# Mixture of experts a slot earlier, with scatters, gathers and additions at places of their own

## What is computed

```
xn = layernorm(x)
x = x + attention(xn)            # 16 heads of 64, causal, softmax of q.k / 8, output projection
      + experts(xn)              # 8 experts, each token goes to its 2 best

gate = softmax(xn @ Wg);  top-2 scores, divided by their sum
expert e: (g * sigmoid(g) * v) @ W2[e]   with g = xn @ W11[e], v = xn @ W12[e]
out  = score0 * expert_out[idx0] + score1 * expert_out[idx1]
```

## Time and profile before

| | |
|---|---|
| time, median of 3 runs | 1510.97 us (1510.51 to 1512.25) |
| the profiled execution's own time | 1510.68 us |
| its span, first to last instruction | 1508.8 us |
| granted TensorE clock, mean | 0.943 |
| DMA moved over the span | 36.23 MB, mean 24 GB/s |
| POOL's indirect DMAs | 32 scatters (median 971 ns on POOL), 32 gathers (median 997 ns) |

### The profile page before, as it was taken

One profiled execution on the slowest core, in us unless ns is written; L12 is line 12 of the kernel. 1 busy time (PEld: TensorE's weight loads), 2 busy tenths in 40 slices (PEclk: granted clock), 3 DMA queues, 4 the chain that ended last, 5 costly groups with the idle time before them and its releaser, 6 DMA issues.

```text
span 1508.8 us, 26916 instructions
## 1 busy us (share of the span) xinstructions
PE 1322.1 (88%) x9090; PEld 1007.4 (67%) x9090; DVE 1080.6 (72%) x3370; ACT 762.2 (51%) x1645; POOL 286.5 (19%) x393
## 2 busy tenths in 40 slices
PE   3289999999999999889977948699999999999961
PEld 2167777777777676656555727577888888888751
DVE  3688888989898887462258836478777787777643
ACT  2325465555546464543324525366666666666540
POOL 4000000000000000000033245322222222222224
PEclk9679999999999999989988978899999999999986
DMA  2000000000000000100003010200111111210002
GB/s 96 0 1 1 2 1 1 1 2 2 1 1 2 1 1 1 44 1 0 0 0 84 1 63 24 69 1 1 58 57 57 57 57 57 57 57 8 17 20 56
DMA packets 39538, 36.23 MB, mean 24 GB/s; under 512 B 2288, under 2 KB 38128, under 8 KB 39152
## 3 DMA queue, kind: packets, MB, share of 16 engines
q1 hardware_dynamic: 37360, 30.36, 6.7%
q0 software_dynamic: 2048, 4.20, 1.0%
HBM read 26.17 MB, written 8.39 MB: 23 GB/s over the span
## 4 chain that ended last, share of the span: by engine, by line
PE 47%; issue 6%; DVE 3%; POOL 3%; DMA 2%; ACT 1%; another core or an unknown queue 1%; SPq 0%; POOLq 0%; DVEq 0%; ACTq 0%
PE PS L2182 8%; PE PS L2168 8%; PE PS L2109 4%; PE PS L2160 4%; PE PS L2161 4%; PE PS L2195 4%; PE PS L2202 3%; PE PS L2239 2%; PE PS L2129 2%; PE PS L1804 2%; PE PS L2210 2%; PE PS L2249 1%; PE PS L2009 1%; PE PS L2027 1%
## 5 line engine op out<-in xcount | busy, mean ns | idle before, releaser
L1035 ACT ACTIVATE pe_<-PS 128x512 f32<-128x512 f32 (+3 forms) x384 | 177.6, 488 | 160.1 <-PE PS L2012 119.3
L1102 ACT ACTIVATE PN<-PS,NM 128x128 f32<-128x128 f32 (+7 forms) x256 | 189.0, 739 | 109.7 <-DVE NM L1708 69.3
L1708 DVE CUSTOM_DVE_ANT_0 PS<-PS,mask_row 128x128 f32<-128x128 f32 (+7 forms) x256 | 194.2, 765 | 67.0 <-PE PS L2161 58.8
L2160 PE MATMUL PS<-KA,QA 128*128 128x512 f32 (+3 forms) x384 | 159.0, 415 | 55.9 <-issue 41.0
L2168 PE MATMUL PS<-ident,PN 128*128 128x128 f32 x1152 | 179.1, 278 | 9.1 <-issue 2.6
L2168 PEld LDWEIGHTS PS<-ident,PN 128*128 128x128 f32 x1152 | 137.0, 143 | 48.3 <-issue 36.8
L1989 PE MATMUL PS<-kta,qta 128*128 128x512 f32 (+3 forms) x384 | 148.2, 421 | 5.7 <-DVE tmqs L1421 2.3
L2009 PE MATMUL PS<-qtb,kta 128*128 128x512 f32 (+3 forms) x384 | 138.9, 389 | 0.9 <-ACT pe_ L1035 0.9
L2161 PE MATMUL PS<-KB,QA 128*128 128x512 f32 (+3 forms) x384 | 130.7, 353 | 0.0
L1421 DVE CUSTOM_DVE_ANT_0 PS<-PS,W 128x128 f32<-128x128 f32 (+3 forms) x256 | 124.8, 496 | 3.6 <-PE PS L1989 2.2
L2160 PEld LDWEIGHTS PS<-KA,QA 128*128 128x128 f32 x384 | 75.2, 196 | 71.9 <-issue 52.4
(11 more groups left out here) (294 smaller groups left out, 2919.4 us busy)
## 6 DMA issues: line engine op xcount, KB each, us to landing
W<-w SPq DMA_DIRECT2D x40, 384.0 KB, 4.1
W<-by_expert SPq DMA_DIRECT2D x10, 256.0 KB, 4.7
expert_out<-YS SPq DMA_DIRECT2D x10, 256.0 KB, 2.3
W<-w SPq DMA_DIRECT2D x1, 2508.0 KB, 10.9
by_expert<-WOZ SPq DMA_DIRECT2D x2, 1024.0 KB, 6.8
W<-w SPq DMA_DIRECT2D x1, 1536.0 KB, 5.8
X<-x SPq DMA_DIRECT2D x2, 512.0 KB, 4.9
out<-X SPq DMA_DIRECT2D x1, 1024.0 KB, 5.0
```

The lines of the kernel that those rows point to most:

```text
L1035: act.activation(pe_[:, h, n % 2, 0:w], PS[:, 4 + h % 2, 0:w], ACT.Exp, scale=HD0 ** -0.5)\
L1102: act.activation(prob_rows(u, r), scores_of(u), ACT.Exp, bias=NM[:, u:u + 1], scale=-1.0, accum_out=SM[:, r % 2, u:u + 1]).then_inc(score_ ...
L1708: dve.tensor_tensor_reduce(scores_of(u), scores_of(u), mask_row[:, S - w:S], -HD1 ** -0.5, -MASKED, ALU.add, ALU.min, NM[:, u:u + 1]).then ...
L2160: pe.matmul(piece, query, KA[:, b, h, lo:lo + n], start=True, stop=False)
```

## The change

The expert batches run from slot 4 instead of 5. The router starts in slot -1 (`gate0+`) and makes four steps after each item instead of one. The scatters are an item `send0` at the end of POOL's order, in three portions of 12, 12 and 8, in the slots 1, 2 and 3, each with one wait for the landing of all so far. The gathers are an item `fetch0'`: sixteen for batch 0 of the tokens in slot 14, sixteen for batch 1 in slot 15, each portion with waits for all its landings. The second half of `YG` lies over the expert weights, so no gather waits for additions. The additions are items `cm0'` to `cm7'` of DVE in slot 16, each with four additions (two tiles, first halves and then second halves). The result is stored in two DMAs of 512 KB.

```diff
-        YG = XM
+        YG = [XM, W1[:, lo_:lo_ + NT * D].rearrange("p (t d) -> p t d", t=NT)]
-        PE1 = steps1("gate0 S0 T14.1' md0' ... S7 gate1' k1+ T5.0 ...
+        PE1 = steps1("S0 T14.1' md0' ... S7 k1+ gate0+ T5.0 S8 T4.0 T6.0 v1+ S9 mu2 S10 gate1 w6' T7.0 w4' ...
-        DVE1 = steps1("gate0 mx13' x0' tc11.1' x2' mx14' mx15' ql1 zc1' mx0 mx1 qr1+ kd1 mx2 kr0+ mx3 tc15.1' mh1 mx5 "
-                     "tc0.0 mx4 gate1 tc1.0 ql0+ zc2' mx6 mh0 mx7 mx8 gate2' tc6.0 kd0+ mx9 mh2 x6' mx10 x4' mx11 "
-                     "tc9.1 tc9.0 mx12 mh3")
+        DVE1 = steps1("mx13' x0' tc11.1' x2' mx14' mx15' cm0' ql1 zc1' cm1' mx0 mx1 qr1+ kd1 mx2 gate1 kr0+ mx3 tc15.1' "
+                     "cm2' mh1 mx5 tc0.0 mx4 tc1.0 ql0+ zc2' cm3' cm4' cm5' mx6 mh0 mx7 mx8 tc6.0 kd0+ gate0+ mx9 mh2 "
+                     "x6' cm7' mx10 x4' cm6' mx11 gate2 tc9.1 tc9.0 mx12 mh3")
-        POOL1 = steps1("kh1' qh1' kh0 qh0 kl0 kl1'")
+        POOL1 = steps1("kh1' qh1' kh0 qh0 kl0 kl1' send0 fetch0'")
-        MOE_FROM, BATCHES, DISPATCH_FROM = 5, TILES1 // 4, 3
+        MOE_FROM, BATCHES = 4, TILES1 // 4
+        ROUTER_STEPS = 4
+        SENDS = [12, 12, 8]
+        ONCE = {"send": range(MOE_FROM - 3, MOE_FROM), "fetch": range(MOE_FROM + BATCHES - 1, MOE_FROM + BATCHES + 1),
+                "cm": (ROUNDS - 1,)}
+            def send(n):
+                pool.wait_ge(routed, 1)
+                pool.wait_ge(slots_cleared, 48)
+                upto = sum(SENDS[0:n + 1])
+                for i in range(sum(SENDS[0:n]), upto):
+                    pool.indirect_dma_start(... XM[:, i // 2, :] ...).then_inc(dispatched, 16)
+                pool.wait_ge(dispatched, 16 * upto)
+            def fetch(b):
+                pool.wait_ge(y_stored, 16 * BATCHES)
+                for t in range(TB * b, TB * (b + 1)):
+                    for k in range(2):
+                        pool.indirect_dma_start(YG[b][:, 2 * (t % TB) + k, :], ... ).then_inc(fetched[t], 16)
+                for t in range(TB * b, TB * (b + 1)):
+                    pool.wait_ge(fetched[t], 32)
+                elif kind == "cm":
+                    for t in (2 * item[1], 2 * item[1] + 1):
+                        after(dve, ("x", t % TB // 2 * 2), ROUNDS - 2 + t // TB)
+                        dve.wait_ge(fetched[t], 32)
+                        dve.scalar_tensor_tensor(X[:, t, :], YG[t // TB][:, 2 * (t % TB), :], w_two[:, t, 0:1], X[:, t, :],
+                                                 ALU.mult, ALU.add).then_inc(half_combined, 1)
+                    for t in (2 * item[1], 2 * item[1] + 1):
+                        halves[0] += 1
+                        dve.wait_ge(half_combined, halves[0])
+                        dve.scalar_tensor_tensor(... 2 * (t % TB) + 1 ...).then_inc(combined[t // TB], 1)
+                for _ in range(ROUTER_STEPS):
+                    if not held:
+                        held = next(router, None) in ("exp", "prefix")
+            for b in range(B):
+                sp.wait_ge(combined[b], TB)
+                sp.dma_start(out[b * S:(b + 1) * S, :] ..., X[:, b * TB:(b + 1) * TB, :]).then_inc(stored, 16)
```

More of the change, by code:

```diff
@@ L519, in rounds @@
                         if r == 0:
+                            yield item, r
+                    elif item[0] in ONCE:
+                        if r in ONCE[item[0]]:
                             yield item, r
@@ L542, in program @@
             sem("m1_tokens_by_act"), sem("m1_tokens_by_dve"), sem("m1_out_by_act"), sem("m1_out_by_dve"))
-        slots_cleared, dispatched, y_stored, combined = (
-            sem("m1_slots_cleared"), sem("m1_dispatched"), sem("m1_out_stored"), sem("m1_combined"))
+        slots_cleared, dispatched, y_stored, half_combined = (
+            sem("m1_slots_cleared"), sem("m1_dispatched"), sem("m1_out_stored"), sem("m1_half_combined"))
+        combined = two("m1_combined")
         weights_in, tokens_in = two("m1_weights_in"), two("m1_tokens_in")
-        fetched = [sem(f"m1_fetched_{k}") for k in range(8)]
+        fetched = [sem(f"m1_fetched_{t}") for t in range(NT)]
         done1 = {}
@@ L552, in counts @@
             for item, r in rounds(steps):
-                if item[0] == "gate":
+                if item[0] == "gate" or item[0] in ONCE:
                     continue
@@ L753, in _ @@
                          YS[:, :].rearrange("p (c d) -> p c d", c=4)).then_inc(y_stored, 16)
-            sp.wait_ge(combined, 2 * NT)
-            sp.dma_start(out.rearrange("(t p) d -> p t d", p=P), X[:, :, :]).then_inc(stored, 16)
-            sp.wait_ge(stored, 16)
+            for b in range(B):
+                sp.wait_ge(combined[b], TB)
+                sp.dma_start(out[b * S:(b + 1) * S, :].rearrange("(t p) d -> p t d", p=P), X[:, b * TB:(b + 1) * TB, :])                    .then_inc(stored, 16)
+            sp.wait_ge(stored, 32)
         @block.gpsimd
@@ L899, in _ @@
                 link(pool.memset(KB[head_rows(1 - h), :, h, :].bitcast(F32), 0.0))
-            def dispatch():
+            def send(n):
                 pool.wait_ge(routed, 1)
                 pool.wait_ge(slots_cleared, 48)
-                for t in range(NT):
-                    for k in range(2):
[L907 to L914, removed]
+                upto = sum(SENDS[0:n + 1])
+                for i in range(sum(SENDS[0:n]), upto):
+                    pool.indirect_dma_start(
+                        by_expert[:, :], bass.IndirectOffsetOnAxis(idx[:, i // 2, i % 2:i % 2 + 1], 0), XM[:, i // 2, :],
+                        None, bounds_check=SLOTS - 1, oob_is_err=False).then_inc(dispatched, 16)
+                pool.wait_ge(dispatched, 16 * upto)
+            def fetch(b):
+                pool.wait_ge(y_stored, 16 * BATCHES)
+                for t in range(TB * b, TB * (b + 1)):
+                    for k in range(2):
+                        pool.indirect_dma_start(YG[b][:, 2 * (t % TB) + k, :], None, expert_out[:, :],
+                                                bass.IndirectOffsetOnAxis(idx[:, t, k:k + 1], 0),
+                                                bounds_check=SLOTS - 1, oob_is_err=False).then_inc(fetched[t], 16)
+                for t in range(TB * b, TB * (b + 1)):
+                    pool.wait_ge(fetched[t], 32)
             for item, r in rounds(POOL1):
                 kind = item[0]
-                if r >= DISPATCH_FROM:
+                if kind in ("send", "fetch"):
                     after(pool, *last)
-                    next(sending, None)
+                    if kind == "send":
+                        send(r - ONCE[kind][0])
+                    else:
+                        fetch(r - ONCE[kind][0])
+                    continue
                 last = item, r
@@ L945, in _ @@
                     pool.wait_ge(wo_zero, 1)
[L947 to L955, removed]
         @block.scalar
@@ L1677, in _ @@
             router, held = gate(1, E1, wt1), True
+            halves = [0]
             for item, r in rounds(DVE1):
@@ L1681, in _ @@
                     held = False
+                elif kind == "cm":
[7 more added lines that the diff above has]
+                        dve.wait_ge(half_combined, halves[0])
+                        dve.scalar_tensor_tensor(X[:, t, :], YG[t // TB][:, 2 * (t % TB) + 1, :], w_two[:, t, 1:2],
+                                                 X[:, t, :], ALU.mult, ALU.add).then_inc(combined[t // TB], 1)
                 elif kind == "mc":
```

6 lines of the change are left out of this document (3 added, 3 removed).

## The result

The changed kernel takes 1519.21 us, median of 5 runs (1517.78 to 1521.52), against 1511.44 (5 runs, 1510.51 to 1512.25) before: ratio 1.0054, 95% interval 1.0039 to 1.0069. It is slower by some 8 us. The profiled execution took 1521.52, its span is 1519.8 us, 11.0 longer than before.

A forecast was written before the change was run, and what follows sets the result against it. GpSimd's queue, not its busy time, was taken to hold TensorE and VectorE. Terms -40.6 + 0.7 + 14.3 + 1.5 + 31.4 + 0 - 20.4 - 0.7 = -13.8 from 1510.68 gave 1497 us, range 1486 to 1513.

The forecast's parts named there:

- router, above bare slots: Slots 0 and 1: router costs 7.9 us now; squeezed into fewer items, +1.5 more, from -3 to +8.
- send0's wait: First twelve scatters wait for `routed`, so ql1 ahead of slot 1 starts 16.3 us late; +14.3, from 10 to 19.
- send1 and send2 beside attention: Later scatter portions of 12 and 8 on GpSimd's queue: send1 0.7 us late, +0.7; send2 in time, 0.
- fetch0's wait: First sixteen gathers wait for the last expert store, so VectorE waits 33.4 us at ql1, slot 14; +31.4, from 26 to 36.
- fetch1 beside attention: Second sixteen gathers, slot 14's second half: pays the 12.7 us that slot 15 no longer does; 0 against before.
- Scatters, slots 2 and 3, -40.6: Slots of 62.4 and 50.8 us lose their stalls when scatters move, down to bare 36.3 each; -40.6 us.
- The waits at ql1: VectorE waits for GpSimd's casts behind send0 and fetch0: 16.3 and 33.4 us, each less 3 absorbed, plus 1 for the clock.
- a rival at +6.5: Squeezed router starves TensorE, where S4 to S8 need VectorE most; 1503 us, chance 0.08.
- The tail: Kernel's end: twelve additions hide, last ends at 1484.4 instead of 1503.27, smaller last store; -20.4 us, from -16 to -22.
- GpSimd's queue stops TensorE outright: Nothing absorbed in the two waits, lower clock, no TensorE work beside fetch1; +18.6, 1515 us, slower; chance 0.14.
- Slot 15's stretch is its own: The 12.7 us stay in slot 15, not caused by gathers; slot 14 pays 7.4 for the queue; 1504 us, chance 0.11.
- The cheap gathers: Gathers hardly slow slot 14's second half, only the queue counts; -5.3, 1492 us, chance 0.07.

The follow-up runs named there:

- router alone: Kernel before with only the router's part of the change: gate0 in slot -1, gate1 and gate2 at new places, four steps an item; 1506.82 us, ratio 0.9968.
- the two kernels with the scatters in the gap: Changed kernel with sixteen scatters behind qh1 in each of two slots: gathers a slot later, 1505.93 us; pauses after fours, gathers behind the last cast, 1455.76 us.
- the ruler: Kernel before with useless DMAs or memsets added behind qh1 in five otherwise repeating slots, three kernels; 1549.26, 1553.84 and 1533.27 us, the last with the sixteen scatters.
- the gap experiment: Changed kernel with gathers one slot later and scatters as two unpaused portions of 16 behind qh1, where GpSimd idles; 1505.93 us, ratio 0.9954.
- the slot above: Slot 5 of the kernel before with useless DMAs added, here twelve scatters in one string behind qh1; the string cost 11.4 us, whole kernel 1549.26 us.

## Why the prediction was wrong

It said 1497 and a range to 1513, faster; it came out at 1519, slower. On the spans: 1495.0 predicted, 1519.8 measured. The difference of 24.8 us by its own terms:

| term | predicted | measured | difference |
|---|---|---|---|
| router, above bare slots | 7.9 + 1.5 | 13.6 (50.0 + 36.2 - 72.6, router alone) | +4.2 |
| send0's wait | 14.3 | 16.0 (66.03 - 50.01) | +1.7 |
| send1 and send2 beside attention | 0.7 | 11.1 + 6.6 (47.31 - 36.21, 42.91 - 36.3) | +17.0 |
| fetch0's wait | 31.4 | 32.8 (72.73 - 39.93) | +1.4 |
| fetch1 beside attention | 12.7 | 16.5 (52.79 - 36.3) | +3.8 |
| slot 15 to the end | 55.4 | 52.7 | -2.7 |
| slot 3, and the start of slot 0 | 0 | +0.1, 0.7 earlier | -0.6 |

The bare 36.3 for slot 14 is the 39.93 of before less the 3.6 by which slots 4 and 5 grew, since the batches moved a slot. The 55.4 is 89.2 before, less 12.7, 20.4 and 0.7. One split in the table is uncertain. Slot 0 without send0's wait is 50.01 us with the router alone, but 52.38 and 52.40 in the two kernels with the scatters in the gap, where the last 24 value matmuls of the slot run at the lower clock (4.24 us at 838.59, for 2.60 at 839.04 with the router alone). By these the router costs 16.0 and the wait 13.6; the sum of the two rows stays.

- **The step that failed is the cost of send1 and send2: "0.7 us late, +0.7" and "30 us, in time, 0".** They were costed as time in GpSimd's queue alone, and as such the sum was right: no wait at ql1 in slots 1 and 2. But a string of twelve costs 11.4 and of eight 6.15 by itself, with no queue involved, and here they cost 11.1 and 6.6. This alone is 17.0 of the 24.8 us and more than the whole predicted gain of 13.8. The prediction had the evidence one paragraph further on: it wrote that gathers beside attention are not free, read 12.7 us from slot 15, and did not ask the same of the scatters. The earlier trace rows explain why the scatters had never shown it: the kernel before issued them in fours and waited for each four. Removing that wait looked like removing a cost; it was what kept the scatters cheap.
- **Scatters, slots 2 and 3, -40.6: right** as what the old places cost. Slot 3 is 36.38, and slot 2 less the 6.15 of a string of eight is 36.8.
- **The waits at ql1: right in place and length.** 16.42 and 32.91 us measured, 16.3 and 33.4 worked out from the earlier trace rows. The discount of 3 for work absorbed was wrong for the long wait: 32.8 us of slot time were lost to it. For the short one it stays open: 16.0 were lost if the router alone is the base, 13.6 if the kernels with the scatters in the gap are.
- **The router: wrong size.** The reasoning that four steps an item starve PE between mx2 and mx4 was set down as a rival at +6.5; the router alone measured +5.7. Two steps in place of four gave 48.90 + 36.58 = 85.5 us for slots 0 and 1, for 52.40 + 38.24 = 90.6 with four, each with twelve paused scatters in slot 1.
- **fetch1: right in kind, small in size.** 12.7 came from slot 15's stretch, where part of the string was hidden; the ruler gives 17.0 for sixteen, the slot 16.5.
- **The tail: right.** From the first row maximum of slot 15 to the end 52.7 us, 2.7 less than summed. Its last additions end at 1516.16, its store 3.6 us later (3.9 estimated).

**The rivals.** "GpSimd's queue stops TensorE outright" got the time, 1515, and the sign nearest, but by luck: its mechanism is another. Its place was the two waits and fetch1, and it said nothing of slots 1 and 2; the gap experiment shows the loss with an empty queue. "Slot 15's stretch is its own" is refuted twice: its second 384-wide to second 640-wide maximum takes 7.80 us in the changed kernel (1473.76 to 1481.56), where before took 21.77, and with gathers in fours beside it the stretch is as short. The cheap gathers are refuted by slot 14.

The prediction weighed a rule of the Trainium skill: "SBUF — State Buffer", section "SBUF: two separate sides", says that engine and DMA ports are disjoint. In so far as it is about moving data the runs agree: 12 DMAs of 64 KB cost 0.0 us, and 512, 256 or 4 bytes a row make 11.4, 11.4 and 12.6. It can't be read as saying that no DMA slows an engine: strings of indirect DMAs do, whatever the way is. The prediction gave that reading 0.11 and counted the gathers' 12.7 us against it, so the failed step doesn't come from there.

**What stays open.** The traces show that in a string TensorE's results are taken up late by ScalarE and VectorE. TensorE itself goes on for as long as it has work in its order, and what ScalarE finishes is taken up at once (its copy ends at 1051.56 in the slot above, and TensorE goes on at 1051.69). The time isn't lost inside VectorE's instructions either: its busy time in the slot is 31.66 us with the string and 31.66 without cost. Whether the signal, or the end of the matmul itself, is what is late can't be told: PE's ends are modelled. Why GpSimd's issue should hold it, and why only from the fifth DMA on, wasn't shown by any run. Whether it is that the DMAs are indirect, or that GpSimd takes 1.28 us to issue each, isn't separated: the plain ones were over in 6.5 us, and a string of plain DMAs as long in time wasn't run.

## What to carry to other kernels

Before a wait between DMAs is taken out, ask what else it does. Issue indirect DMAs from GpSimd in groups of at most four with about 2 us between them, and put them where neither GpSimd's next casts nor anything behind them are due; either alone gave little here (-3.7 us for the pauses, -13 to -15 us for the places), both together 63 us. (The gathers' places weren't quite the same: without pauses the first sixteen still stood ahead of two casts.) And a cost read in one place (a stretch that doubles while gathers run) belongs to every other operation of its kind that the change moves.

## What the runs showed of the hardware

- Indirect DMAs of GpSimd back to back, 1.28 us apart (gathers 1.30): up to four cost attention 0.6 us, each further one about 1.4 us. Twelve scatters of 4, 256 or 512 bytes a row cost 12.6, 11.4 and 11.4 us, twelve gathers of 512 bytes 11.9. Beside other slots of this kernel a string of sixteen cost 15.4 to 17.8.
- Twelve plain DMAs of 64 KB from the same engine: 0.54 us from one to the next, 6.5 us in all, no cost.
- A pause of about 2 us after each four takes the cost away (0.7 to 1.1 us left for twelve), whether spent waiting for the landing or on small memsets. Pausing only after six leaves 5.6 us.
- The granted clock fell from 1.00 (2.4 GHz) to 0.50 inside the stall of such a string, after TensorE had run out of work, and was 0.90 on average over the slot; it added to the loss and did not start it.
